# Attention maxima from score products of 32 rows per head, two heads side by side on TensorE

## The chip, the cores and the metric

The kernel runs on one core of a Trainium2 chip. The metric is the device time of one execution in microseconds (us). The core has TensorE for matrix products (PE; its weight loads are shown apart as PEld), VectorE (DVE), ScalarE (ACT), GpSimd (POOL) and SyncE (SP), which here issues all transfers. Engines run on their own and wait for each other through semaphores; each engine works through its own instructions in order, and SP's DMA issues are such instructions too.

## The reference, cut to what matters

```python
x = x + attention(layernorm(x))      # changed here
x = x + fp4_ffn(layernorm(x))
x = x + state_space(layernorm(x))
x = x + mixture_of_experts(layernorm(x))
# attention, x: (2, 1024, 128), 16 heads of 8 channels, rotary q and k
attn = jnp.einsum('bhqd,bhkd->bhqk', q, k) * scale
attn = jax.nn.softmax(attn, axis=-1)
out = jnp.einsum('bhqk,bhkd->bhqd', attn, v)
```

A softmax comes out the same whatever number is subtracted from a row's scores before the exponential, as long as it is near enough to the row's maximum.

## The kernel before, in words

q and k are split into three bf16 parts each and stored in DRAM (q_dram, k_dram). A stack of 72 rows, 3 x 3 pairs of parts x 8 channels, gives a float32-like score from one bf16 product; rows 72 to 95 of the stack add the negated row maximum, which is written into the stack of q later.

Attention runs in eight passes (PASSES), each of four heads (QUAD) of one batch entry, 1024 queries by 1024 keys. A pass has 16 steps (STEPS): two halves of the queries by eight key tiles of 128. In a step PE makes four transposed score products (L1310, keys on the partitions, 512 queries), ACT takes their exponentials (L738), and PE makes the value products of the step before (L1327; four heads, 16 columns each, side by side; float32, so each is two instructions).

The maxima for pass it+1 are made during pass it. Between the four products of a step PE puts the score products for two tiles (score_half, L1291; a tile is 128 queries of a head by 1024 keys, two products of 512), and DVE reduces each tile from two banks of PSUM (L970). Two tiles are in flight: PE waits for s_max before it overwrites banks. After 16 tiles DVE splits the 16 maxima into two bf16 parts and transposes them (L974 to L979), and SP writes them into the q stack with four small DMAs (store_maxima, L512). PE waits for them (s_nrow) ahead of step 0 for the first half and ahead of step 8 for the second. Before pass 0 the same tiles are made with nothing between them.

The stacks have three sets (SETS); set p is loaded again when its pass is over (load, L500 to L506: two loads into qs, six into ks and one small one). SP's queue in a pass is: maxima store for the next pass's first half; output store; wait for the end of the pass (s_pv); load; output store; maxima store for the next pass's second half. At the head of the program the stores of the first four part tiles are followed by the loads of all three sets, the other four part stores, and then the maxima stores of pass 0. After pass 5 SP goes on with load_out(0): the denominators den of the first batch entry, which DVE inverts (L987) ahead of its reductions for pass 7 (those that run during pass 6).

Of the kernel before, what the change touches and what calls it, by code (L numbers as in the profile page):

```python
# [14 lines left out]
BF16 = mybir.dt.bfloat16  # L15
F32R = mybir.dt.float32r
I32 = mybir.dt.int32
ALU = mybir.AluOpType
ACT = mybir.ActivationFunctionType
AX = mybir.AxisListType  # L20

P = 128
BATCH = 2
SEQ = 1024
# [3 lines left out]
BANK = 512  # L28
# [4 lines left out]
HD = D // HEADS  # L33
QUAD = 4
PASSES = BATCH * HEADS // QUAD
# [7 lines left out]
STEPS = 2 * KT  # L43
MAX_TILES = 2
SETS = 3
# [19 lines left out]
def build_kernel(nc, i, out):  # L65
# [3 lines left out]
    def sb(name, shape, dt=F32):  # L69
        return ctx.enter_context(nc.sbuf_tensor(name, shape, dt))  # L70

    def sem(name):
        return ctx.enter_context(nc.semaphore(name))

    with ctx:
        ps = ctx.enter_context(nc.psum_tensor("ps", [P, 8, BANK], F32))
# [4 lines left out]
        sq = sb("sq", [P, TILES, D])  # L81
# [42 lines left out]
        fill = sb("fill", [4 * (ROWS - PROD), 2, 2 * BANK], BF16)  # L124
        stacks = [[sb(f"{w}{n}", [ROWS, 2, QUAD, BANK], BF16) for w in ("qs", "ks")] for n in reversed(range(SETS))][::-1]
        qs, ks = ([pair[n] for pair in stacks] for n in range(2))
        prob = sb("prob", [P, 8, BANK])
        vq = [sb(f"vq{n}", [P, KT, QUAD, VW]) for n in range(SETS)]
        v = sb("v", [P, PASSES, KT, QC])
# [3 lines left out]
        bv_all = sb("bv_all", [P, D])  # L133
        bo_all = sb("bo_all", [P, D])
        nmax = sb("nmax", [P, 2, 16])
        nmax_p = sb("nmax_p", [P, 32], BF16)
        nmax_t = sb("nmax_t", [P, 2, 32], BF16)
        o_sb = sb("o_sb", [P, 2, BANK])
        den = sb("den", [P, BATCH, HEADS * SEQ // P])
        rden = sb("rden", [P, BATCH, SEQ])  # L140
        num = sb("num", [P, TOKENS])
        phase.close()

# [50 lines left out]
        q_dram = nc.dram_tensor("q_dram", (PASSES, 2, PARTS, QC, BANK), BF16, kind="Internal").ap()  # L194
# [30 lines left out]
        s_fill = sem("s_fill")  # L225
        s_set = sem("s_set")
        s_qk = [sem(f"s_qk{n}") for n in range(SETS)]
        s_score = sem("s_score")
        s_max = sem("s_max")
        s_nmax = sem("s_nmax")  # L230
# [113 lines left out]
        def norm_dve_var(k, h):  # L344
            a, b = h * TILES // 2, (h + 1) * TILES // 2
            nc.vector.wait_ge(s_squared, 2 * k + h + 1)
            nc.vector.tensor_reduce(stat[:, 2, a:b], sq[:, a:b, :], AX.X, ALU.add).then_inc(s_var, 1)  # L347

        def norm_dve_scale(k, h):
            a, b = h * TILES // 2, (h + 1) * TILES // 2  # L350
            u = 2 * k + h
            nc.vector.wait_ge(s_rstd, u + 1)
            nc.vector.wait_ge(s_centred, u + 1)
            nc.vector.tensor_tensor(xc[:, a:b, :], xc[:, a:b, :], bc(stat[:, 3, a:b], D),
                                    ALU.mult).then_inc(s_normed, 1)
# [81 lines left out]
        N_W34 = 3 + 16 + 6  # L437

        LOADS = 16 * (2 * (PARTS + 1) + 1)

        @block.sync
        def _(sp):
# [44 lines left out]
            def store_parts(u):  # L487
# [4 lines left out]
                for g in range(QUAD):  # L492
                    sp.dma_start(dst[4 * (c // 2) + g, c % 2].rearrange("n c t -> c n t"),
                                 parts[QC * g:QC * g + QC, u % CHUNKS]).then_inc(s_parts_out[u % CHUNKS], 16)

            def load(it, p):

                for f in range(2):

                    sp.dma_start(qs[p][0:PROD, f], q_dram[bass.ds(it, 1), f].rearrange(  # L500
                        "o n (d h) t -> (o n d) (h t)", h=QUAD).unsqueeze(1).to_broadcast([PARTS * HD, PARTS, QUAD * BANK])).then_inc(s_qk[p], 16)
                    for a in range(PARTS):
                        sp.dma_start(ks[p][HD * PARTS * a:HD * PARTS * (a + 1), f], k_dram[bass.ds(it, 1), f].rearrange(
                            "o n (d h) t -> d (o n) (h t)", h=QUAD)).then_inc(s_qk[p], 16)

                sp.dma_start(qs[p][PROD:PROD + 2], fill[0:16, 0, 0:BANK]).then_inc(s_qk[p], 16)  # L506
# [17 lines left out]
                sp.wait_ge(s_parts_out[n], 16 * QUAD)  # L524
            sp.wait_ge(s_set, 16 * 2 * SETS)
            for p in range(SETS):
                load(p, p)
            for u in range(CHUNKS, 2 * CHUNKS):
                store_parts(u)
# [5 lines left out]
            def one_pass(it, p, more, again=None):  # L535
                if more:
                    store_maxima(it + 1, (p + 1) % SETS, 0)
                store_out(it, 0)
                if again is not None:
                    sp.wait_ge(s_pv, STEPS * (it + 1))  # L540
                    load(again, p)
                store_out(it, 1)
                if more:
                    store_maxima(it + 1, (p + 1) % SETS, 1)
# [385 lines left out]
        def _(dve):  # L930
# [33 lines left out]
            def maxima(it):  # L964

                for half in range(2):
                    for n in range(16):
                        t = 16 * half + n
                        dve.wait_ge(s_score, 32 * it + t + 1)
                        nc.vector.tensor_reduce(nmax[:, half, n:n + 1], ps[:, 2 * (t % 2):2 * (t % 2) + 2, :],  # L970
                                                AX.XY, ALU.max, negate=True).then_inc(s_max, 1)
                    w = 2 * (2 * it + half)
                    dve.wait_ge(s_max, 32 * it + 16 * half + 16)
                    nc.vector.tensor_copy(nmax_p[:, 0:16], nmax[:, half]).then_inc(s_mstep, 1)  # L974
                    dve.wait_ge(s_mstep, w + 1)
                    nc.vector.tensor_tensor(nmax_p[:, 16:32], nmax[:, half], nmax_p[:, 0:16], ALU.subtract).then_inc(s_mstep, 1)
                    dve.wait_ge(s_mstep, w + 2)
                    dve.wait_ge(s_nrow[half], 64 * it)
                    nc.vector.transpose(nmax_t[:, half, :], nmax_p[:]).then_inc(s_nmax, 1)  # L979

# [25 lines left out]
            dve.wait_ge(s_res, 2)  # L1006
            norm_dve_a(1, 0)
            dve.wait_ge(s_qk[SETS - 1], LOADS * (PASSES // SETS + 1))
            quant(0, wf[:], wfq[:], (s_wf, 16 * 5), scaled=lambda: norm_dve_var(1, 0), before_last=lambda: norm_dve_scale(1, 0))
            quant(1, x_half(xc, 0), x_half(sq, 0), (s_normed, 3))  # L1010

# [241 lines left out]
        def _(pe):  # L1253
# [29 lines left out]
                                          start=True, stop=True)  # L1283
                mm.then_inc(s_v_ps, 1)

            def score_half(it, p, t, kk):

                half, h, q = t // 16, t % 16 // 4, t % 4
                if kk == 0 and not (isinstance(it, int) and it == 0 and t < 2):
                    pe.wait_ge(s_max, 32 * it + t - 1)  # L1290
                mm = nc.tensor.matmul(ps[:, 2 * (t % 2) + kk], qs[p][:, half, h, q * P:(q + 1) * P],  # L1291
                                      ks[p][:, kk, h, :], start=True, stop=True)
                if kk == 1:
                    mm.then_inc(s_score, 1)

            def one_pass(it, p, first, more, loads=None, between={}):
                for s in range(STEPS):
                    if s in between:
                        between[s]()
                    half, kt = divmod(s, KT)  # L1300
                    if kt == 0:
                        pe.wait_ge(s_nrow[half], 64 * (it + 1))
                    if more and s == 0:
                        pe.wait_ge(s_qk[(p + 1) % SETS], LOADS * loads)
                    todo = [(MAX_TILES * s + n // 2, n % 2) for n in range(2 * MAX_TILES)] if more else []
                    for j in range(QUAD):
                        n = 4 * s + j
                        if n >= 3:
                            pe.wait_ge(s_exp, 4 * STEPS * it + n - 2)
                        nc.tensor.matmul(ps[:, 4 + (first + n) % 3], ks[p][:, kt // 4, j, kt % 4 * P:(kt % 4 + 1) * P],  # L1310
                                         qs[p][:, half, j, :], start=True, stop=True).then_inc(s_st, 1)
                        for t, kk in todo[len(todo) * j // 4:len(todo) * (j + 1) // 4]:
                            score_half(it + 1, (p + 1) % SETS, t, kk)
                        if s >= 1 and j == (QUAD - 1 if more else QUAD - 2):
                            products(it, p, s - 1)
                products(it, p, STEPS - 1)
# [11 lines left out]
                                          start=(kt == 0), stop=(kt == KT - 1))  # L1328
                mm.then_inc(s_pv, 1)

            pe.wait_ge(s_qk[0], LOADS)
            pe.wait_ge(s_v, 4)
            for t in range(32):
                score_half(0, 0, t, 0)
                score_half(0, 0, t, 1)
            with pe.Fori(0, PASSES // SETS) as r:
                for p in range(SETS):
                    one_pass(SETS * r + p, p, 4 * STEPS * p, True, r + 1 + (p + 1) // SETS)
            one_pass(PASSES - 2, 0, 0, True, PASSES // SETS + 1)

            def project_out(b):

# [68 lines left out]
                pe.wait_ge(s_wft, 3)  # L1411
                turn_x(1, 1)

            one_pass(PASSES - 1, 1, 4 * STEPS, False, between={1: lambda: project_out(0), 8: turn_weights, 12: turn_first_x})
            pe.wait_ge(s_wft, 3)
            for p in range(4):
                gate_up(p)
# [239 lines left out]
```

## Time and profile before

| | |
|---|---|
| median of 3 runs | 1059.84 us (1059.75 to 1062.03) |
| the profiled execution | 1058.78 us, span 1057.0 us |
| busy | PE 82%, DVE 82%, ACT 54%, POOL 23% of the span |
| attention | from about 41 us (first load of a stack) to 471 us |

The span is from the first to the last instruction. A timeline row shows start, duration, engine, line and operation, how many instructions are merged into it, and in brackets the engine's idle time ahead of it with what ended it. A matmul's duration is modelled and overlaps its successors: for the rate of PE one reads the distance between starts. Rows with SPq are DMA issues in SP's queue, the time that SP needs to hand the transfer over, not the transfer itself.

### The profile page before, as it was taken

The numbers are of one execution on the slowest core, as the hardware profiler recorded it, in microseconds if no ns is written. First come the engines' busy times: TensorE is split into PE (matmuls) and PEld (weight loads), VectorE is DVE, ScalarE is ACT, GpSimd is POOL, SyncE is SP. The second block draws the span as 40 slices with busy tenths as digits, with TensorE's granted clock in tenths as the row PEclk, the third lists the DMA queues.
The fourth block names the chain that finished last, engine by engine and source line by source line (L and its number), as shares of the span: only waits on it lengthen the run. The fifth ranks groups of instructions, "written<-read, shape, count | busy, mean of one in ns | idle before, by whom it ended". The sixth has DMA issues, their size and how long they took to land. (4 is left out here: it accounts for less than half of the span.)

```text
span 1057.0 us, 12554 instructions
## 1 busy us (share of the span) xinstructions
PE 862.0 (82%) x3703; PEld 392.3 (37%) x3703; DVE 862.0 (82%) x795; ACT 572.5 (54%) x897; POOL 238.8 (23%) x131
## 2 busy tenths in 40 slices
PE   5589999989999949985464457777777579999998
PEld 2212222222222212224342222222222266888886
DVE  6698888878888748828956899999999873888886
ACT  2304777767777737882131642332333165888885
POOL 3700000000000000100110156776777620123110
PEclk9857999999999979998677788998999867999999
DMA  7440020110101030003000233444444002122111
GB/s 174 128 132 1 11 56 24 54 58 12 56 11 57 14 99 11 11 20 85 0 1 0 89 119 118 160 158 140 158 159 158 21 1 83 60 97 83 60 60 41
DMA packets 37977, 73.51 MB, mean 70 GB/s; under 512 B 7299, under 2 KB 21627, under 8 KB 36891
## 3 DMA queue, kind: packets, MB, share of 16 engines
q1 hardware_dynamic: 37922, 72.82, 21.7%
q8 instruction: 30, 0.49, 0.2%
q14 instruction: 25, 0.20, 0.1%
HBM read 62.50 MB, written 8.85 MB: 68 GB/s over the span
## 5 line engine op out<-in xcount | busy, mean ns | idle before, releaser
L970 DVE TENSOR_REDUCE nmax<-ps 128x1 f32<-128x1024 f32 x256 | 301.0, 1218 | 57.3 <-PE ps L1291 57.3
L738 ACT ACTIVATE prob<-ps 128x512 f32<-128x512 f32 x512 | 265.7, 605 | 137.1 <-PE ps L1310 136.8
L1291 PE MATMUL ps<-ks,qs 96*128 96x512 bf16 x512 | 206.3, 416 | 29.7 <-DVE nmax L970 18.1
L1310 PE MATMUL ps<-qs,ks 96*128 96x512 bf16 x512 | 194.7, 389 | 7.0 <-ACT prob L738 3.3
L670 POOL TENSOR_TENSOR hc<-hst,cbr 128x1024 f32<-128x1024 f32 x64 | 153.4, 2398 | 93.1 <-DVE hst L1107 93.1
L1489 PE MATMUL ps<-hc,ident 128*128 128x512 f32 x256 | 134.4, 650 | 41.7 <-POOL hc L670 38.8
L862 ACT ACTIVATE ps<-dt,a_neg 128x1024 f32<-128x1024 f32 x64 | 71.5, 1118 | 145.9 <-DVE hst L1107 145.9
L1107 DVE TENSOR_TENSOR_SCAN hst<-ps,dbx 128x1024 f32<-128x1024 f32 x64 | 145.6, 2276 | 0.0
L1327 PE MATMUL ps<-prob,vq 128*16 128x512 f32 x1024 | 133.6, 598 | 0.8 <-ACT prob L738 0.7
L1174 DVE TENSOR_TENSOR act_l<-act_t,act_h 128x1024 fp32r<-128x1024 f32 x64 | 92.1, 1449 | 35.5 <-ACT act_h L903 35.5
L1310 PEld LDWEIGHTS ps<-qs,ks 96*128 96x128 bf16 x512 | 49.6, 98 | 164.6 <-ACT prob L738 117.5
L899 ACT ACTIVATE act_t<-ps,b_now 128x512 f32<-128x512 f32 x128 | 82.8, 683 | 24.1 <-PE ps L1531 24.1
L1489 PEld LDWEIGHTS ps<-hc,ident 128*128 128x128 f32 x256 | 47.1, 202 | 106.6 <-POOL hc L670 67.8
L1291 PEld LDWEIGHTS ps<-ks,qs 96*128 96x128 bf16 x512 | 48.9, 101 | 100.8 <-DVE nmax L970 53.0
L1096 DVE TENSOR_TENSOR dbx<-dtx,ps 128x1024 f32<-128x1024 f32 x64 | 76.3, 1193 | 3.2 <-PE ps L1476 3.1
L903 ACT ACTIVATE act_h<-act_t 128x1024 fp32r<-128x1024 f32 x64 | 67.9, 1061 | 2.0
L644 POOL COPY vq<-v 128x256 f32<-128x256 f32 x8 | 3.1, 403 | 272.8 <-PE ps L1327 272.8
L377 POOL TENSOR_SCALAR stat<-stat 128x8 f32<-128x8 f32 x8 | 4.2, 525 | 265.2 <-DVE stat L347 265.1
L1476 PE MATMUL ps<-bcp,sel_b 128*128 128x512 bf16 x128 | 41.2, 405 | 21.5 <-DVE dbx L1096 19.7
L1529 PE MATMUL ps<-xh,w_l 128*128 128x512 f32 x128 | 51.7, 404 | 0.0
L1530 PE MATMUL ps<-xl,w_h 128*128 128x512 f32 x128 | 51.2, 400 | 0.0
L1531 PE MATMUL ps<-xh,w_h 128*128 128x512 f32 x128 | 51.1, 400 | 0.0
(176 smaller groups left out, 969.7 us busy)
## 6 DMA issues: line engine op xcount, KB each, us to landing
cbr<-s_dram SPq DMA_DIRECT2D x64, 512.0 KB, 3.6
gate<-c_dram SPq DMA_DIRECT2D x8, 1024.0 KB, 6.7
qs<-q_dram SPq DMA_DIRECT2D x18, 288.0 KB
ks<-k_dram SPq DMA_DIRECT2D x54, 96.0 KB
o_dram<-o_sb SPq DMA_DIRECT2D x16, 256.0 KB, 2.1
wf<-in_L_ffn_w SPq DMA_DIRECT2D x8, 256.0 KB, 2.8
wfq<-in_L_ffn_w SPq DMA_DIRECT2D x8, 256.0 KB, 3.1
q_dram<-parts SPq DMA_DIRECT2D x16, 96.0 KB, 2.1
```

The costliest lines, as they stand in the source:

```text
L670: nc.gpsimd.tensor_tensor(hc[:, slot], hst[:, slot], cbr[:, slot], ALU.mult).then_inc(s_hc, 1)
L738: nc.scalar.activation(prob[:, n % 8], ps[:, 4 + (first + n) % 3], ACT.Exp, scale=ATT_SCALE).then_inc(s_exp, 1)
L862: nc.scalar.activation(abar(slot), dt[:, b * SEQ:(b + 1) * SEQ], ACT.Exp, scale=a_neg[:, bass.ds(n, 1)]).then_inc(s_abar, 1)
L899: nc.scalar.activation(act_t[:, u % 2, h], ps[:, h], ACT.Gelu, bias=b1_now[:, u // CHUNKS, h:h + 1]).then_inc(s_gelu, 1)
L970: nc.vector.tensor_reduce(nmax[:, half, n:n + 1], ps[:, 2 * (t % 2):2 * (t % 2) + 2, :], AX.XY, ALU.max, negate=True).then_inc(s_max, 1)
L1096: nc.vector.tensor_tensor(dbx[:, slot].rearrange("p (k t) -> p k t", k=2), dtx[:, b * SEQ:(b + 1) * SEQ].rearrange("p (k t) -> p k t", k=2 ...
L1107: nc.vector.tensor_tensor_scan(hst[:, slot], abar(slot), dbx[:, slot], 0.0, ALU.mult, ALU.add).then_inc(s_scan, 1)
L1174: nc.vector.tensor_tensor(act_l[:, u % 2, h:h + 2], act_t[:, u % 2, h:h + 2], act_h[:, u % 2, h:h + 2].bitcast(F32), ALU.subtract).then_in ...
L1291: mm = nc.tensor.matmul(ps[:, 2 * (t % 2) + kk], qs[p][:, half, h, q * P:(q + 1) * P], ks[p][:, kk, h, :], start=True, stop=True)
L1310: nc.tensor.matmul(ps[:, 4 + (first + n) % 3], ks[p][:, kt // 4, j, kt % 4 * P:(kt % 4 + 1) * P], qs[p][:, half, j, :], start=True, stop=T ...
L1327: mm = nc.tensor.matmul(ps[32 * j:32 * j + VW, 7], vq[p][:, kt, j, :], prob[:, (4 * s + j) % 8], start=(kt == 0), stop=(kt == KT - 1))
L1489: mm = nc.tensor.matmul(ps[:, 6 + k], ident[:], hc[:, slot, k * BANK:(k + 1) * BANK], start=first, stop=last)
```

## The change

The products from which the maxima are made use only the two leading parts of q and k: 2 x 2 pairs x 8 channels = 32 rows for a head. They get operands of their own, qm and km (128 partitions, four heads of 32 rows under one another). score_pair makes two products, for two heads that lie on neighbouring groups of 32 rows of TensorE, into two banks; DVE reduces each bank for itself (two maxima for each reduction), and the two halves of the keys are joined by one further small operation. The scores that go into the exponential still come from the stacks of 96 rows. The order of tiles changes from head by head to query tile by query tile.

The operands come by a new function load_heads: for each half of the sequence and each head one DMA into km and two into qm, 24 in all, ahead of each load. PE waits for s_qm instead of s_qk ahead of the maxima's products, and for s_qk at the start of a pass. rden takes the place of sq, to make room.

```diff
+        qm, km = ([sb(f"{w}{n}", [P, 2, BANK], BF16) for n in range(SETS)] for w in ("qm", "km"))
+            def load_heads(it, p):
+
+                for f in range(2):
+                    for h in range(QUAD):
+                        q, k = (t[bass.ds(it, 1), f].rearrange("o n (d h) t -> (o n d) h t", h=QUAD)[0:2 * HD, h]
+                                for t in (q_dram, k_dram))
+                        sp.dma_start(km[p][32 * h:32 * h + 32, f], k.unsqueeze(0).to_broadcast([2, 2 * HD, BANK])).then_inc(s_qm[p], 16)
+                        for a in range(2):
+                            sp.dma_start(qm[p][32 * h + 16 * a:32 * h + 16 * a + 16, f],
+                                         q[HD * a:HD * a + HD].unsqueeze(0).to_broadcast([2, HD, BANK])).then_inc(s_qm[p], 16)
...
             for p in range(SETS):
+                load_heads(p, p)
                 load(p, p)
...
                     sp.wait_ge(s_pv, STEPS * (it + 1))
+                    load_heads(again, p)
                     load(again, p)
...
-                        nc.vector.tensor_reduce(nmax[:, half, n:n + 1], ps[:, 2 * (t % 2):2 * (t % 2) + 2, :],
-                                                AX.XY, ALU.max, negate=True).then_inc(s_max, 1)
+                        nc.vector.tensor_reduce(nmax_k[:, half, kk, 2 * pair:2 * pair + 2, qt], ps[:, 2 * pair:2 * pair + 2, :],
+                                                AX.X, ALU.max, negate=True).then_inc(s_max, 1)
...
+                    nc.vector.tensor_tensor(nmax[:, half], nmax_k[:, half, 0].rearrange("p h q -> p (h q)"),
+                                            nmax_k[:, half, 1].rearrange("p h q -> p (h q)"), ALU.min).then_inc(s_mstep, 1)
...
-                mm = nc.tensor.matmul(ps[:, 2 * (t % 2) + kk], qs[p][:, half, h, q * P:(q + 1) * P],
-                                      ks[p][:, kk, h, :], start=True, stop=True)
+                for n in range(2):
+                    rows = slice(32 * (2 * pair + n), 32 * (2 * pair + n + 1))
+                    mm = nc.tensor.matmul(ps[:, 2 * pair + n], qm[p][rows, half, qt * P:(qt + 1) * P],
+                                          km[p][rows, kk, :], start=True, stop=True)
+                mm.then_inc(s_score, 1)
...
-                        for t, kk in todo[len(todo) * j // 4:len(todo) * (j + 1) // 4]:
-                            score_half(it + 1, (p + 1) % SETS, t, kk)
+                        if more and j % 2:
+                            score_pair(it + 1, (p + 1) % SETS, MAX_TILES * s + j // 2)
```

PE, one step inside a pass. Before (L1310 are the four products for the exponentials, L1291 those for the maxima, L1327 the value products):

```order
L1310 MATMUL ps<-qs,ks 128x512 [waits s_exp]
L1290 REGISTER_ALU
L1291 MATMUL ps<-ks,qs 128x512 [waits s_max]
L1309 REGISTER_ALU
L1310 MATMUL ps<-qs,ks 128x512 [waits s_exp]
L1291 MATMUL ps<-ks,qs 128x512
L1327 MATMUL ps<-prob,vq 16x512 [waits s_exp]
L1327 MATMUL ps<-prob,vq 16x512 x3
```

Now (L1333 are the products for the exponentials, L1315 the pair for the maxima, L1350 the value products):

```order
L1333 MATMUL ps<-qs,ks 128x512 [waits s_exp]
L1332 REGISTER_ALU
L1333 MATMUL ps<-qs,ks 128x512 [waits s_exp]
L1312 REGISTER_ALU
L1315 MATMUL ps<-km,qm 128x512 [waits s_max]
L1315 MATMUL ps<-km,qm 128x512
L1350 MATMUL ps<-prob,vq 16x512 [waits s_exp]
L1350 MATMUL ps<-prob,vq 16x512 x3
```

The products for the maxima stood one by one between the others; now two stand together after every second one, and the wait for DVE is ahead of each pair.

SP, from the end of a pass to the store of the second half's maxima. Before:

```order
L500 ISA [waits s_pv]
L500 DMA qs<-q_dram 72x1x2048
L503 DMA ks<-k_dram 24x1x2048 x3
L500 ISA
L500 DMA qs<-q_dram 72x1x2048
L503 DMA ks<-k_dram 24x1x2048 x3
L506 DMA qs<-fill 2x8x512
L518 ISA [waits s_o]
L518 DMA o_dram<-o_sb 128x512
L512 DMA qs<-nmax_t 2x16x32 [waits s_nmax]
L512 DMA qs<-nmax_t 2x16x32 x3
```

Now (the five rows from the second on come eight times, and then what stood there before):

```order
L506 ISA [waits s_pv]
L506 DMA km<-k_dram 32x1x512
L508 DMA qm<-q_dram 16x1x512
L508 ISA
L508 DMA qm<-q_dram 16x1x512
L506 ISA
...
L515 DMA qs<-q_dram 72x1x2048
L518 DMA ks<-k_dram 24x1x2048 x3
...
L533 DMA o_dram<-o_sb 128x512
L527 DMA qs<-nmax_t 2x16x32 [waits s_nmax]
```

24 issues with their register instructions stand between the end of the pass and the nine loads, and so ahead of the maxima's stores too. At the head of the program the same 24 stand ahead of the loads of each of the three sets.

## Rows read from the trace of the kernel before

**Rows 1.** Timeline of PE in one step (start us, us, engine, line, operation, count).
```profile
200.84 0.39 PE L1310 MATMUL ps<-qs,ks 96*128 96x512 bf16 x1
...
202.36 0.38 PE L1291 MATMUL ps<-ks,qs 96*128 96x512 bf16 x1
202.67 1.05 PE L1327 MATMUL ps<-prob,vq 128*16 128x512 f32 x8
203.65 0.39 PE L1310 MATMUL ps<-qs,ks 96*128 96x512 bf16 x1
```

**Rows 2.** Timeline of DVE in the same stretch.
```profile
201.91 2.36 DVE L970 TENSOR_REDUCE nmax<-ps 128x1 f32<-128x1024 f32 x2 [0.46 <-PE ps L1291]
...
204.51 0.18 DVE L976 TENSOR_TENSOR nmax_p<-nmax,nmax_p 128x16 bf16<-128x16 f32 x1
```

**Rows 3.** Timeline of ACT in the same stretch.
```profile
201.27 2.07 ACT L738 ACTIVATE prob<-ps 128x512 f32<-128x512 f32 x4 [0.75 <-PE ps L1310]
```

**Rows 4.** Timeline of PE: first products of passes 1, 2, 3; step 8 of 3.
```profile
135.99 0.39 PE L1310 MATMUL ps<-qs,ks 96*128 96x512 bf16 x1
...
181.54 0.39 PE L1310 MATMUL ps<-qs,ks 96*128 96x512 bf16 x1
...
229.88 0.39 PE L1310 MATMUL ps<-qs,ks 96*128 96x512 bf16 x1 [2.72 <-issue]
...
253.06 0.39 PE L1310 MATMUL ps<-qs,ks 96*128 96x512 bf16 x1
```

**Rows 5.** Timeline of SP's queue after pass 5 (SPq: the issue of a DMA).
```profile
367.93 0.90 SPq L500 DMA_DIRECT2D qs<-q_dram  x1
368.93 2.32 SPq L503 DMA_DIRECT2D ks<-k_dram  x3
371.45 0.81 SPq L500 DMA_DIRECT2D qs<-q_dram  x1
...
375.63 0.35 SPq L518 DMA_DIRECT2D o_dram<-o_sb  x1
376.10 2.67 SPq L512 DMA_DIRECT2D qs<-nmax_t  x4
379.03 0.66 SPq L551 DMA_DIRECT2D den<-o_dram  x1
...
384.67 0.53 SPq L556 DMA_DIRECT2D rden<-r_dram  x1
```

**Rows 6.** Page, parts 3 (packets, MB, share) and 6 (KB, us to landing).
```profile
q1 hardware_dynamic: 37922, 72.82, 21.7%
...
o_dram<-o_sb SPq DMA_DIRECT2D x16, 256.0 KB, 2.1
```

**Rows 7.** Timeline of SP's queue at the head of the program.
```profile
49.07 2.08 SPq L503 DMA_DIRECT2D ks<-k_dram  x3
51.19 0.79 SPq L500 DMA_DIRECT2D qs<-q_dram  x1
...
61.50 1.88 SPq L493 DMA_DIRECT2D q_dram<-parts  x4
...
71.41 0.66 SPq L512 DMA_DIRECT2D qs<-nmax_t  x1
```

**Rows 8.** Timeline of PE: first score product, starts of passes 0 and 6.
```profile
50.76 1.46 PE L1291 MATMUL ps<-ks,qs 96*128 96x512 bf16 x3 [9.67 <-DMA qs<-fill]
...
88.57 0.63 PE L1310 MATMUL ps<-qs,ks 96*128 96x512 bf16 x1
...
367.60 0.39 PE L1310 MATMUL ps<-qs,ks 96*128 96x512 bf16 x1
...
383.46 0.61 PE L1291 MATMUL ps<-ks,qs 96*128 96x512 bf16 x1 [13.70 <-DVE nmax L970]
```

**Rows 9.** Timeline of DVE after pass 5.
```profile
381.37 0.95 DVE L987 RECIPROCAL den<-den 128x128 f32<-128x128 f32 x1 [13.35 <-DMA den<-o_dram]
```

**Rows 10.** Page, part 2: granted clock in tenths, 40 slices.
```profile
PEclk9857999999999979998677788998999867999999
```

More of the change, by code:

```diff
@@ L135, in build_kernel @@
         nmax = sb("nmax", [P, 2, 16])
+        nmax_k = sb("nmax_k", [P, 2, 2, QUAD, 4])
         nmax_p = sb("nmax_p", [P, 32], BF16)
@@ L139, in build_kernel @@
         den = sb("den", [P, BATCH, HEADS * SEQ // P])
-        rden = sb("rden", [P, BATCH, SEQ])
+        rden = sq[:].rearrange("p (b t) c -> p b (t c)", b=BATCH)
         num = sb("num", [P, TOKENS])
@@ L227, in build_kernel @@
         s_qk = [sem(f"s_qk{n}") for n in range(SETS)]
+        s_qm = [sem(f"s_qm{n}") for n in range(SETS)]
         s_score = sem("s_score")
@@ L439, in build_kernel @@
         LOADS = 16 * (2 * (PARTS + 1) + 1)
+        HEAD_LOADS = 16 * 2 * 3 * QUAD
         @block.sync
@@ L967, in maxima @@
                     for n in range(16):
-                        t = 16 * half + n
-                        dve.wait_ge(s_score, 32 * it + t + 1)
-                        nc.vector.tensor_reduce(nmax[:, half, n:n + 1], ps[:, 2 * (t % 2):2 * (t % 2) + 2, :],
-                                                AX.XY, ALU.max, negate=True).then_inc(s_max, 1)
-                    w = 2 * (2 * it + half)
+                        u = 16 * half + n
+                        qt, kk, pair = n // 4, n % 4 // 2, n % 2
+                        dve.wait_ge(s_score, 32 * it + u + 1)
+                        nc.vector.tensor_reduce(nmax_k[:, half, kk, 2 * pair:2 * pair + 2, qt], ps[:, 2 * pair:2 * pair + 2, :],
+                                                AX.X, ALU.max, negate=True).then_inc(s_max, 1)
+                    w = 3 * (2 * it + half)
                     dve.wait_ge(s_max, 32 * it + 16 * half + 16)
+                    nc.vector.tensor_tensor(nmax[:, half], nmax_k[:, half, 0].rearrange("p h q -> p (h q)"),
+                                            nmax_k[:, half, 1].rearrange("p h q -> p (h q)"), ALU.min).then_inc(s_mstep, 1)
+                    dve.wait_ge(s_mstep, w + 1)
                     nc.vector.tensor_copy(nmax_p[:, 0:16], nmax[:, half]).then_inc(s_mstep, 1)
-                    dve.wait_ge(s_mstep, w + 1)
+                    dve.wait_ge(s_mstep, w + 2)
                     nc.vector.tensor_tensor(nmax_p[:, 16:32], nmax[:, half], nmax_p[:, 0:16], ALU.subtract).then_inc(s_mstep, 1)
-                    dve.wait_ge(s_mstep, w + 2)
+                    dve.wait_ge(s_mstep, w + 3)
                     dve.wait_ge(s_nrow[half], 64 * it)
@@ L1284, in _, with score_pair, one_pass @@
                 mm.then_inc(s_v_ps, 1)
[L1286 to L1290, printed above, removed]
-                mm = nc.tensor.matmul(ps[:, 2 * (t % 2) + kk], qs[p][:, half, h, q * P:(q + 1) * P],
-                                      ks[p][:, kk, h, :], start=True, stop=True)
-                if kk == 1:
-                    mm.then_inc(s_score, 1)
-            def one_pass(it, p, first, more, loads=None, between={}):
+            def score_pair(it, p, u):
+                half, qt, kk, pair = u // 16, u % 16 // 4, u % 4 // 2, u % 2
+                if not (isinstance(it, int) and it == 0 and u < 2):
+                    pe.wait_ge(s_max, 32 * it + u - 1)
+                for n in range(2):
[3 more added lines that the diff above has]
+                mm.then_inc(s_score, 1)
+            def one_pass(it, p, first, loads, more, between={}):
+                pe.wait_ge(s_qk[p], LOADS * loads)
                 for s in range(STEPS):
@@ L1303, in one_pass @@
                     if more and s == 0:
-                        pe.wait_ge(s_qk[(p + 1) % SETS], LOADS * loads)
-                    todo = [(MAX_TILES * s + n // 2, n % 2) for n in range(2 * MAX_TILES)] if more else []
+                        pe.wait_ge(s_qm[(p + 1) % SETS], HEAD_LOADS * (loads + (p + 1) // SETS))
                     for j in range(QUAD):
@@ L1329, in products @@
                 mm.then_inc(s_pv, 1)
-            pe.wait_ge(s_qk[0], LOADS)
+            pe.wait_ge(s_qm[0], HEAD_LOADS)
             pe.wait_ge(s_v, 4)
-            for t in range(32):
-                score_half(0, 0, t, 0)
-                score_half(0, 0, t, 1)
+            for u in range(32):
+                score_pair(0, 0, u)
             with pe.Fori(0, PASSES // SETS) as r:
                 for p in range(SETS):
-                    one_pass(SETS * r + p, p, 4 * STEPS * p, True, r + 1 + (p + 1) // SETS)
-            one_pass(PASSES - 2, 0, 0, True, PASSES // SETS + 1)
+                    one_pass(SETS * r + p, p, 4 * STEPS * p, r + 1, True)
+            one_pass(PASSES - 2, 0, 0, PASSES // SETS + 1, True)
             def project_out(b):
@@ L1412, in turn_first_x @@
                 turn_x(1, 1)
-            one_pass(PASSES - 1, 1, 4 * STEPS, False, between={1: lambda: project_out(0), 8: turn_weights, 12: turn_first_x})
+            one_pass(PASSES - 1, 1, 4 * STEPS, PASSES // SETS + 1, False, between={1: lambda: project_out(0), 8: turn_weights, 12: turn_first_x})
             pe.wait_ge(s_wft, 3)
```

1 line of the change is left out of this document (added).

## The prediction

> **What bounds the kernel now.** I read the page's slices first (the clock is full through attention but for slice 3 and the stops [rows 10]), then the order of time on PE and DVE in the middle of an attention pass, then SP's own queue around a pass boundary, since the change puts most of its new instructions there.
>
> A steady step of a pass takes 2.81 us on PE (200.84 to 203.65): eight products of 96 rows, then the value products, then the next step's first product [rows 1]. Products in the same mode start 0.217 us apart (200.84 to 202.36 is seven of them). In that stretch PE never sits idle, while DVE waits 0.46 us for PE before each pair of reductions, and its two reductions take 2.36 us [rows 2]. ACT's four exponentials fit easily (2.07 us of work with a wait of 0.75 us for PE ahead of them) [rows 3]. So PE is the bound inside a pass, DVE is 0.46 us behind it, and a shorter PE step is worth something until DVE stops it. A pass is 16 steps, 45.55 us from first product to first product (135.99 to 181.54), and its step 8 comes 22.11 us after its start (181.54 to 203.65) [rows 4, 1].
>
> SP is nobody's bound before, but look at when it is asked. After a pass ends it issues the loads for a set three passes on, and only behind them, in the same queue, the last four stores of the maxima of the pass that is already running. PE needs those at step 8. At the boundary into pass 6, PE starts at 367.60, the loads start at 367.93 and the fourth maxima store is issued at 378.1 (376.10, four in 2.67 us) [rows 8, 5]. A small store lands 2.1 us after its issue, by the o_dram row [rows 6]; so the maxima are there 12.6 us after the start of the pass, 9.5 us before step 8. That slack is what the change spends.
>
> Two places have no slack. At the head of the program the stores of pass 0's maxima stand behind all three sets of loads (first maxima store 71.41) [rows 7]; PE starts pass 0 at 88.57 [rows 8]. And between passes 5 and 6 PE stands 13.70 us, because DVE waits 13.35 us for the denominators, whose load SP issues at 379.03, behind the same loads and stores [rows 8, 9, 5].
>
> **The score products.** 512 products of 96 rows go; 512 of 32 rows come, two at a time on different row groups. If a pair runs side by side, a step has two product slots fewer, 0.43 us. But the pair and its neighbours differ in how they occupy the array. The rows show what a change of mode costs: from the last 96-row product to the value products (16 columns each) 0.31 us instead of 0.22 (202.36 to 202.67) [rows 1], so 0.09 us. The new order alternates two ordinary products, a pair, two ordinary products, a pair; three more changes in a step. Step: 2 x 0.217 (within the ordinary products) + 4 x 0.31 (into or out of a pair) + 0.01 (within the pairs; the value products, eight in 1.05 us, start as close together) + 0.98 (value products to the next step) = 2.66 us, 0.15 less than 2.81. No row shows 32-row products. With no price for the three new changes the step would be 2.39, which is also about where DVE stops it (2.36 us for the two reductions [rows 2]); if the two of a pair ran one after the other, it would be 3.09. I take 2.66.
>
> The Trainium skill (TensorEngine Tiling (Array Packing), Key Properties) says that changing the tiling mode, not just the tile, drains TensorE; that speaks against this order, and the 0.31 above agrees. By TensorE: Matmul & The Clock Gate (Part 3) products on different row groups start some 4 ns apart, which gives 2.66 with the drain and 2.39 without; no row here shows it for rows.
>
> **DVE.** 256 reductions stay, each over 1024 elements, and write two maxima instead of one; same duration. One more small operation for each half pass, 16 in all, like the 0.18 us subtraction [rows 2]. It falls into DVE's 0.46 us of idle time per step, or behind SP; zero. If that cover were gone it would be 3 us.
>
> **The new loads.** Each set gets 24 more DMAs, 8 into km (32 x 512) and 16 into qm (16 x 512), issued ahead of the nine that were there. What an issue costs SP: the ks loads, nearest in form (one row per partition, source dims that don't match the destination's), take 2.12 us for three at the head (49.07 to 51.19), 0.71 each [rows 7], and inside the loop with the address register 2.52 for three (368.93 to 371.45), 0.84 each [rows 5]. So a block of 24 is 17.0 us at the head and 20.2 us in the loop. Bounds: the issue of rden (0.53, where a ks load's alone is 0.67: 2.08 for three with two gaps of 0.04) [rows 5, 7], the part stores (1.88 for four, 0.47) [rows 7] and the o_dram store (0.35) [rows 5] below; the qs loads (0.90) above. I take the ks row.
>
> Head of the program: 3 x 17.0 = 51.0 us on SP. The first maxima store moves from 71.41 to 122.4, the fourth is issued at 124.4 and lands at 126.5. PE's own start slips only by 17.0 instead of 7.2 us (its first product waited for the nine loads until 50.76 [rows 8]), and 88.57 + 9.8 = 98.4 is early enough to be hidden. Pass 0 starts at 126.5 instead of 88.57: **+37.9**.
>
> Pass 0: 15 steps x 0.15: **-2.3** (its first step has no value products, and saves nothing to speak of).
>
> Passes 1, 2, 4, 5: maxima for step 8 land 12.6 + 20.2 = 32.8 us after the start; PE is ready for step 8 at 22.11 - 1.1 = 21.0, so it stands 11.8 us. What is left of the pass is 45.55 - 22.11 - 8 x 0.15 = 22.2 us. After a stop the clock is low for a while: pass 3 starts after a stop at 229.88 and reaches step 8 at 253.06, 23.2 instead of 22.1, so 1.1 us [rows 4]. Period 32.8 + 22.2 + 1.1 = 56.1, against 45.55: +10.55 each, **+42.2**. The saving of the first eight steps is swallowed by the wait.
>
> Pass 3: the same, but the 2.72 us for instructions at the loop's end and the 1.1 behind it [rows 4] lie in the time that is now waited anyway: 10.55 - 3.8, **+6.8**.
>
> Pass 6: its maxima are no trouble, as it already stands. But the denominators' load is issued behind the (unused) loads of pass 5, so DVE, and PE with it, start 20.2 later: 20.2 - 2.3 = **+17.9**.
>
> Pass 7 has no score products, and pass 6 issues no loads: 0. Everything behind attention moves as a block.
>
> Sum: 37.9 - 2.3 + 42.2 + 6.8 + 17.9 = +102.5. The profiled execution took 1058.78 us (span 1057.0): 1161.3. The median of the three runs is 1.1 higher: **1162 us**. 216 new issues lie on the path (72 at the head, 24 at each of six boundaries), so 0.01 us in the price of one is 2.2 us of the result.
>
> **Rivals.**
> Cheap issues: the new DMAs have plain row counts, and cost SP what the part stores or the o_dram store do, 0.2 to 0.32 less than I took. Even then 24 x 0.52 + 12.6 = 25.1 is beyond step 8. 216 x 0.2 = 43, 216 x 0.32 = 69: 1093 to 1119 us.
> Pairs one after the other: 0.43 more in each of 70 steps that count (15 in passes 0 and 6, 8 in the five others): +30, 1192 us.
> Few DMA engines: a block is 512 packets of 1 KB. The program's mean packet is 1.9 KB and holds an engine for 97 ns (21.7% of 16 x 1057 us by 37922) [rows 6]. On sixteen engines that is nothing. If a DMA used only two, it would be 256 packets each: 13 us if time goes with size, hidden behind SP; 25 us if it doesn't, then 7.8 more for each of three blocks and 4.6 for each of six: +51, 1213 us. The skill's page DMA: Bandwidth & Descriptors (How many engines) gives two here, as the source's slowest dimension is the repeated 2; no row shows the number of engines.
> Clock: pauses or half-empty products keep PE at 1.2 GHz after each stop; as it stood at the head, 5 tenths in slice 3 [rows 10]. 70 steps of some 4.9 us: +157, 1318 us. Against it: after the stop before pass 3 it cost 1.1 us in all.
> Faster: if an issue costs 0.27 all in, a block takes 6.5 us, the maxima arrive at 19.1, before step 8 even of a 2.39 us step (22.11 - 7 x 0.42 = 19.2), and the wait of passes 1 to 5 is gone. Then seven passes give 7 x 15 x 0.42 = 44, less 6.4 at the head (71.41 + 19.5 + 4.1 = 95.0) and 6.5 before pass 6: 1028 us. At 0.35 the waits are back with 1.8 + 1.1 us in five passes and the gain is some 10; the sign turns at about 0.39 from start to start. The cheapest row of such a queue is the o_dram store, 0.35 for the issue and 0.46 with the register move before the next [rows 5].
>
> **How the numbers follow.** Forecast 0.68, cheap issues 0.10, pairs in series 0.10, few engines 0.05, clock 0.04, faster 0.03. The forecast's own spread is 1162 less 30 (0.53 for an issue) less 19 (step 2.39), and up some 20 (0.09 more for an issue). The range 1112 to 1195 takes in that, the upper edge of cheap issues and pairs in series. About 0.2% (2 us) is what a measurement can tell; faster by more 0.03, within 0.01, slower 0.96.
>
> **What would show it.** SP: km and qm issues of 0.67 us, and the first maxima store at about 122. PE: a start of pass 0 near 126, stops of some 12 us at step 8 of passes 1, 2, 4 and 5 that end with the maxima's stores, a stop of some 33 us before pass 6; spacings of 0.31 around each pair and almost none in it. DVE waits, where it was nearly the bound. It is wrong if issues are 0.4 us or less, if PE waits at step 8 for nothing, or if pass 0 starts before 110.

## The result, and the profile after

The changed kernel takes 1167.8 us (median; 1163.9 to 1169.9), the kernel before 1060.3 in the same runs: ratio 1.101, 95% interval 1.097 to 1.104. The profiled execution has a span of 1164.2 us against 1057.0. The forecast was 1162 us with a range of 1112 to 1195.

Where the 107.2 us of span went, from the first products of the passes in the two traces:

| stretch | before | after | difference | forecast |
|---|---|---|---|---|
| start of pass 0 | 88.57 | 121.70 | +33.1 | +37.9 |
| pass 0 | 47.42 | 46.94 | -0.5 | -2.3 |
| pass 1 | 45.55 | 56.07 | +10.5 | +10.55 |
| pass 2 (with the loop's end) | 48.34 | 60.02 | +11.7 | +10.55 |
| pass 3 | 46.62 | 55.77 | +9.2 | +6.8 |
| passes 4 and 5 | 91.10 | 115.31 | +24.2 | +21.1 |
| pass 6 | 60.55 | 78.78 | +18.2 | +17.9 |
| from pass 7 to the end | 628.9 | 629.6 | +0.8 | 0 |

First the step on PE, the timeline of two steps of pass 2 (start us, us, engine, line, operation, count); it answers to [rows 1].

```profile
240.39 0.60 PE L1333 MATMUL ps<-qs,ks 96*128 96x512 bf16 x2
240.92 0.39 PE L1315 MATMUL ps<-km,qm 32*128 32x512 bf16 x2
241.24 0.61 PE L1333 MATMUL ps<-qs,ks 96*128 96x512 bf16 x2
241.79 0.39 PE L1315 MATMUL ps<-km,qm 32*128 32x512 bf16 x2
242.10 1.05 PE L1350 MATMUL ps<-prob,vq 128*16 128x512 f32 x8
243.09 0.60 PE L1333 MATMUL ps<-qs,ks 96*128 96x512 bf16 x2
```

The two 32-row products of a pair are given 0.39 us together, as much as one 96-row product alone in [rows 1]: the pair runs side by side. From a pair's start to what follows it is 0.32 us (240.92 to 241.24, 241.79 to 242.10). The step is 2.70 us, against 2.81. DVE in the same stretch still waits for PE, now 0.34 us instead of the 0.46 of [rows 2]:

```profile
241.35 2.36 DVE L988 TENSOR_REDUCE nmax_k<-ps 128x2 f32<-128x1024 f32 x2 [0.34 <-PE ps L1315]
```

SP's queue behind pass 1, cut (it answers to [rows 5]):

```profile
224.99 0.70 SPq L506 DMA_DIRECT2D km<-k_dram  x1
225.80 1.49 SPq L508 DMA_DIRECT2D qm<-q_dram  x2
...
244.34 0.83 SPq L515 DMA_DIRECT2D qs<-q_dram  x1
...
252.29 5.37 SPq L527 DMA_DIRECT2D qs<-nmax_t  x8
```

24 issues take 19.35 us (224.99 to 244.34), and the maxima's stores, four of which pass 2 needs at step 8, begin at 252.29, 27.6 us after the pass began at 224.71. What PE makes of that at step 8 of pass 1, with the stop in brackets; behind it the same instructions at half the clock (granted 0.51 from 199 to 205 us, 1.00 from 205 to 208):

```profile
188.73 1.05 PE L1350 MATMUL ps<-prob,vq 128*16 128x512 f32 x8
199.75 1.03 PE L1333 MATMUL ps<-qs,ks 96*128 96x512 bf16 x2 [9.96 <-DMA qs<-nmax_t]
200.72 0.60 PE L1315 MATMUL ps<-km,qm 32*128 32x512 bf16 x2
201.25 1.03 PE L1333 MATMUL ps<-qs,ks 96*128 96x512 bf16 x2
202.22 0.61 PE L1315 MATMUL ps<-km,qm 32*128 32x512 bf16 x2
202.75 1.91 PE L1350 MATMUL ps<-prob,vq 128*16 128x512 f32 x8
204.60 0.73 PE L1333 MATMUL ps<-qs,ks 96*128 96x512 bf16 x2
```

At the head and ahead of pass 6, timelines of PE, SP and DVE; they answer to [rows 7 to 9]:

```profile
121.70 1.03 PE L1333 MATMUL ps<-qs,ks 96*128 96x512 bf16 x2 [25.65 <-DMA qs<-nmax_t]
```
```profile
117.81 5.23 SPq L527 DMA_DIRECT2D qs<-nmax_t  x8
```
```profile
490.95 0.61 PE L1315 MATMUL ps<-km,qm 32*128 32x512 bf16 x2 [32.51 <-DVE nmax_k L988]
```
```profile
488.86 0.95 DVE L1008 RECIPROCAL den<-den 128x128 f32<-128x128 f32 x1 [32.42 <-DMA den<-o_dram]
```

PE had finished the head's products and stood 25.65 us for stores that SP issued at 117.81 instead of 71.41. The stop that the prediction puts before pass 6 lies inside its first step, in both traces (before: pass 6 starts at 367.60, the stop ends at 383.46; now 455.81 and 490.95); it grew from 13.70 to 32.51 us.

The stores themselves are not slow. Once four of them are issued, PE goes on: the fourth of the eight in the row at 252.29 is issued at about 254.3 and PE's step 8 of pass 2 begins at 256.22; at the head it is about 119.8 and 121.70. Both times 1.9 us, in pass 2 right behind 33 loads.

```profile
256.22 1.03 PE L1333 MATMUL ps<-qs,ks 96*128 96x512 bf16 x2 [10.36 <-DMA qs<-nmax_t]
```

### The profile page after: what moved, and what is told of

Same layout as the page of the kernel before. It is cut to its first block and busy times, and to the rows that moved or that the text cites. A ratio compares the mean times of both kernels' runs of the same rounds, so it can differ in the third digit from the quotient of the medians.

```text
span 1164.2 us, 13027 instructions
## 1 busy us (share of the span) xinstructions
PE 860.2 (74%) x3701; PEld 368.2 (32%) x3703; DVE 865.5 (74%) x811; ACT 572.6 (49%) x897; POOL 238.8 (21%) x131
## 5 line engine op out<-in xcount | busy, mean ns | idle before, releaser
L988 DVE TENSOR_REDUCE nmax_k<-ps 128x2 f32<-128x1024 f32 x256 | 300.7, 1220 | 140.2 <-PE ps L1315 140.2
L1333 PE MATMUL ps<-qs,ks 96*128 96x512 bf16 x512 | 171.8, 411 | 77.4 <-DMA qs<-nmax_t 69.8
L1315 PE MATMUL ps<-km,qm 32*128 32x512 bf16 x512 | 111.5, 435 | 67.7 <-DVE nmax_k L988 49.9
L1350 PE MATMUL ps<-prob,vq 128*16 128x512 f32 x1024 | 142.7, 636 | 0.8 <-ACT prob L755 0.7
L1333 PEld LDWEIGHTS ps<-qs,ks 96*128 96x128 bf16 x512 | 39.6, 98 | 245.4 <-issue 124.9
L1315 PEld LDWEIGHTS ps<-km,qm 32*128 32x128 bf16 x512 | 24.4, 93 | 169.0 <-issue 81.1
L1498 PE MATMUL ps<-bcp,sel_b 128*128 128x512 bf16 x126 | 40.8, 406 | 22.2 <-DVE dbx L1118 20.0
```

The source lines that it names most:

```text
L988: nc.vector.tensor_reduce(nmax_k[:, half, kk, 2 * pair:2 * pair + 2, qt], ps[:, 2 * pair:2 * pair + 2, :], AX.X, ALU.max, negate=True).the ...
L1315: mm = nc.tensor.matmul(ps[:, 2 * pair + n], qm[p][rows, half, qt * P:(qt + 1) * P], km[p][rows, kk, :], start=True, stop=True)
L1350: mm = nc.tensor.matmul(ps[32 * j:32 * j + VW, 7], vq[p][:, kt, j, :], prob[:, (4 * s + j) % 8], start=(kt == 0), stop=(kt == KT - 1))
```

## The experiments

The theory: the loss is nothing but SP's issue time of the new DMAs at three kinds of place (head, step 8, denominators), while the products themselves gain a little, as far as the changes of mode let them. Rivals: the products or the low clock carry the loss; the transfers and not their issue do; the 0.3 us beside a pair are not the change of mode. Each run was timed beside the kernel before.

### The loads alone

The kernel before, with operands, load_heads and its calls of the change, and nobody reading them.

```diff
             for p in range(SETS):
+                load_heads(p, p)
                 load(p, p)
...
+                    load_heads(again, p)
                     load(again, p)
```

> The kernel before with the 24 new DMAs issued ahead of each load of a set, into operands that nobody reads; the score products stay as they were. Theory (the loss is SP's issue time ahead of the maxima's stores and the denominators): pass 0 starts at about 122 us instead of 88.6, passes 1, 2, 4, 5 take 57.7 us each (stores land 31.9 us after their start, then 23.4 us of steps and 2.4 us of low clock), the stop before pass 6 is 33 us; about 1171 us, even a little more than the changed kernel, as the steps stay at 2.81 us. Rival (the 32-row products or the clock carry a good part of the loss): well under 1150 us.

Measured: 1165.9 us, ratio 1.101 (1.097 to 1.104). Pass 0 starts at 120.96, pass 1 takes 56.83 us (not the 57.7 forecast, as the issues take 0.81 instead of 0.84; passes 4 and 5 take 57.6 and 58.0), and PE's stop at its step 8 reads:

```profile
188.75 0.38 PE L1309 MATMUL ps<-ks,qs 96*128 96x512 bf16 x1
189.06 1.05 PE L1345 MATMUL ps<-prob,vq 128*16 128x512 f32 x8
199.18 0.60 PE L1328 MATMUL ps<-qs,ks 96*128 96x512 bf16 x1 [9.07 <-DMA qs<-nmax_t]
199.58 0.63 PE L1309 MATMUL ps<-ks,qs 96*128 96x512 bf16 x1
```

The whole loss is there without one 32-row product, and the low clock behind the stop comes with 96-row products too (granted 0.61 from 199 to 205 us). The rival of the products falls.

### The products alone

The changed kernel without the DMAs; qm and km hold a constant, so that the maxima of the rows are left out.

```diff
-                load_heads(p, p)
...
-                    load_heads(again, p)
...
+            for t in (*qm, *km):
+                ins = nc.gpsimd.memset(t[:], 1.375)
```

> The changed kernel without any of the new DMAs: qm and km are filled once with a constant, so the subtracted maxima are not the rows' own; every product, reduction and store of maxima is made as in the change. Theory: steps of 2.70 instead of 2.81 us, no stops at step 8, the head and the stop before pass 6 as in the kernel before: 7 passes x 1.45 us and some 2 us in the head, about 1048 us. Rival (changing the mode costs nothing by itself, the 0.31 us are waits for something that the loads delay): steps of 2.4 us, about 1016 us. Rival (the products lose time of their own): 1060 us or more.

Measured: 1053.5 us, ratio 0.995 (0.992 to 0.997). The direction is that of the theory and neither rival's; the size is 6.4 instead of 12 us. Steps are 2.70 us and pass 1 takes 43.90 instead of 45.55; pass 0 keeps nothing of that (47.39 against 47.42 us), since its first steps ran at the low clock for longer (two steps of 3.0 and 4.85 us and 3.25 for the third, against 3.4, 3.7 and 2.8 before). In the trace, the fastest of the ten executions, pass 7 starts at 420.63 instead of 428.15, 7.5 us earlier. Of the 0.11 us that a step saves, step 9 of a pass gives 0.10 back: it takes 2.98 us at full clock and without a stop, against 2.88 before.

```profile
190.53 0.60 PE L1333 MATMUL ps<-qs,ks 96*128 96x512 bf16 x2
191.07 0.39 PE L1315 MATMUL ps<-km,qm 32*128 32x512 bf16 x2
191.39 0.61 PE L1333 MATMUL ps<-qs,ks 96*128 96x512 bf16 x2
191.94 0.39 PE L1315 MATMUL ps<-km,qm 32*128 32x512 bf16 x2
192.25 1.05 PE L1350 MATMUL ps<-prob,vq 128*16 128x512 f32 x8
193.24 0.60 PE L1333 MATMUL ps<-qs,ks 96*128 96x512 bf16 x2
```

The spacings are those of the changed kernel though no new DMA runs: they belong to PE.

### Stores ahead of loads

```diff
-                if again is not None:
-                    sp.wait_ge(s_pv, STEPS * (it + 1))
-                    load_heads(again, p)
-                    load(again, p)
                 store_out(it, 1)
                 if more:
                     store_maxima(it + 1, (p + 1) % SETS, 1)
+                if again is not None:
+                    sp.wait_ge(s_pv, STEPS * (it + 1))
+                    load_heads(again, p)
+                    load(again, p)
```

> The changed kernel; at a pass's end SP stores the output and the second half's maxima first and issues the 24 new and 9 old loads behind them. Theory: the stops at step 8 go with the low clock behind them, 12.5 us in each of passes 1, 2, 4, 5 and about 7.5 in pass 3, while the head and the stop before pass 6 stay: about 1110 us. Rival (the transfers themselves, not their issue, hold the stores back): the stops stay in part and the time is above 1140 us.

Measured: 1106.1 us, ratio 1.044 (1.040 to 1.047). The bytes are the same and so is the number of DMAs; only who stands behind whom differs. SP's queue behind pass 0 and PE at step 8 of pass 1 (191.24), without a stop:

```profile
171.54 2.63 SPq L527 DMA_DIRECT2D qs<-nmax_t  x4
174.46 0.69 SPq L506 DMA_DIRECT2D km<-k_dram  x1
```
```profile
190.26 1.05 PE L1350 MATMUL ps<-prob,vq 128*16 128x512 f32 x8
191.24 0.60 PE L1333 MATMUL ps<-qs,ks 96*128 96x512 bf16 x2
```

Passes 1, 4 and 5 take 43.9 us each (pass 1: 170.17 to 214.07), no more than in the products alone, though all the new transfers run in them. Pass 3 takes 49.3 against 46.4 there, with a granted clock of 0.52 from 260 to 274 us behind the stop at the loop's end; why it stayed low for longer is open. 62 us of the 107 were this place. By itself the new order would also have freed stores that stood behind transfers and not behind issues; that rival falls by the 1.9 us from issue to PE in the changed kernel, shown above.

### The head's order

```diff
+            load_heads(0, 0)
+            load(0, 0)
+            load_heads(1, 1)
+            sp.wait_ge(s_qk[0], LOADS)
+            store_maxima(0, 0, 0)
+            load(1, 1)
+            store_maxima(0, 0, 1)
             for u in range(CHUNKS, 2 * CHUNKS):
                 store_parts(u)
+            load_heads(2, 2)
+            load(2, 2)
```

> The changed kernel; at the head SP issues only what pass 0 needs (set 0, and the new operands of set 1) ahead of pass 0's maxima stores, and the rest behind. Theory: pass 0 starts at about 97 us, when the head's reductions are through, instead of 121.7: about 1143 us. Rival (PE's pass 0 waits for something else there, such as the transfers): no more than 10 us gained, 1158 us or more.

Measured: 1144.5 us, ratio 1.080 (1.076 to 1.084). Pass 0 starts at 95.44, right behind the last product of the head:

```profile
93.77 0.60 PE L1319 MATMUL ps<-km,qm 32*128 32x512 bf16 x2 [0.52 <-DVE nmax_k L992]
94.91 0.61 PE L1319 MATMUL ps<-km,qm 32*128 32x512 bf16 x2 [0.53 <-DVE nmax_k L992]
95.44 1.03 PE L1337 MATMUL ps<-qs,ks 96*128 96x512 bf16 x2
```

The start of pass 0 comes 26.3 us earlier than in the changed kernel, and 23 us of the whole came back by order alone (1167.8 to 1144.5). The 6.9 us that are left of the 33.1 go with the later first product, 59.3 instead of 50.8, for which the first block has to be issued anyway.

### Half the loads

As the loads alone, with `for h in range(2)` in load_heads: 12 new DMAs a block.

> The kernel before with 12 instead of 24 unread new DMAs ahead of each load (those of two heads). Theory (issue time against a slack): in the loop 12 issues are 9.7 us, the stores land 22.3 us after the start of the pass against step 8 at 22.1, so passes 1 to 5 lose next to nothing; the head loses about 11 us and the stop before pass 6 grows by 9.7: about 1081 us. Rival (each DMA costs its share wherever it stands): half the loss of the 24, about 1113 us.

Measured: 1078.5 us, ratio 1.017 (1.014 to 1.019). Half of the DMAs cost a sixth of the 24's loss (17 of 106 us). PE has no stop at step 8 in any of passes 1 to 5, which together take 231.7 us against 231.6 before. What is lost lies where there was no slack: in the trace pass 6 starts 9.6 us later, and its first two steps take 30.24 instead of 20.28 us. The cost is not one for each DMA; it starts where the slack ends.

### The new DMAs off SP's queue

GpSimd issues all blocks but the 16 DMAs that the head's first products need; SP stores maxima first, the loads after pass 5 that nobody reads are gone, and the first denominators are fetched after pass 4. SP's loop over the passes is written out, so that its addresses are constants.

```diff
+            def heads(it, p):
+                for f in range(2):
+                    heads_k(nc.gpsimd, it, p, f, s_qm[p])
+                    heads_q(nc.gpsimd, it, p, f, s_qm[p])
...
+            for it in range(SETS, PASSES):
+                pool.wait_ge(s_pv, STEPS * (it - SETS + 1))
+                values(it, it % SETS)
+                heads(it, it % SETS)
```

> The change with its new DMAs taken off SP's queue: GpSimd, idle in attention, issues them (SP only the 16 that the head's first products need). SP stores the maxima ahead of loads, the loads that nobody reads after pass 5 are gone, and the first denominators are fetched a pass earlier. Theory (only SP's issue time cost something): no stops at step 8 or before pass 6, pass 0 starts at about 91 us, steps of 2.70 us: the 1053.5 us of the products alone, less 15 for the stop before pass 6, plus some 1.5 at the head: about 1040 us. Rival (the transfers, or GpSimd's slower issue, cost time themselves): 1050 us or more.

Measured: 1037.9 us, ratio 0.978 (0.974 to 0.982), faster than both kernels. Pass 0 starts at 89.81. GpSimd's own timeline at the head:

```profile
46.84 4.68 POOL L456 DMA_DIRECT2D qm<-q_dram  x8
51.45 0.46 POOL L671 COPY vq<-v 128x256 f32<-128x256 f32 x1
51.80 2.39 POOL L450 DMA_DIRECT2D km<-k_dram  x4
```

An issue took it 0.58 us (4.68 by 8), no more than SP's. The passes between the stops take what they take in the products alone (pass 1: 43.90), so neither the transfers nor GpSimd's issues cost anything there.

### The same queue for the kernel before

Only the new order, the dropped loads, the earlier denominators and the written-out loop, none of the change. At the head two sets and not one are loaded ahead of the maxima's stores, as pass 0 reads both.

> The kernel before with the same order of SP's queue (maxima stores ahead of loads, no unread loads, first denominators fetched a pass earlier), nothing of the change. Theory: only the stop before pass 6 goes, 15 us with the low clock behind it: about 1045 us, so the change's products are worth 5 to 7 us over it. Rival (the order of the queue is what helps at other places too): under 1040 us, and no gain is left for the products.

Measured: 1043.4 us, ratio 0.982 (0.979 to 0.986). So three quarters of what the version above gains over the kernel before has nothing to do with the change. In the trace the first two steps of pass 6 take 5.35 instead of 20.28 us. The change is worth 5.5 us between the two medians; the intervals of the two ratios overlap, but the slowest of the four executions with the change (1040.7 us) is faster than the fastest of the four without (1042.2 us).

### One change of mode more, one less

Both on GpSimd's queue. One more: the pairs stand after the first and the third ordinary product.

```diff
-                        if more and j % 2:
+                        if more and j % 2 == 0:
```

> As the one with GpSimd's queue, but the pairs stand after the first and the third ordinary product: six changes of mode in a step instead of five, the same products. Theory (each change costs PE 0.09 us): steps of 2.79 us, +9.5 us, about 1049 us. Rival (the 0.31 us next to a pair is the pair's own length, not the change): steps of 2.70 us, no difference to 1040 us.

Measured: 1046.1 us, ratio 0.985 (0.981 to 0.989), 8.2 us more than with five changes. The step:

```profile
195.05 0.39 PE L1354 MATMUL ps<-qs,ks 96*128 96x512 bf16 x1
195.37 0.39 PE L1336 MATMUL ps<-km,qm 32*128 32x512 bf16 x2
195.69 0.60 PE L1354 MATMUL ps<-qs,ks 96*128 96x512 bf16 x2
196.23 0.39 PE L1336 MATMUL ps<-km,qm 32*128 32x512 bf16 x2
196.55 0.39 PE L1354 MATMUL ps<-qs,ks 96*128 96x512 bf16 x1
196.87 1.05 PE L1371 MATMUL ps<-prob,vq 128*16 128x512 f32 x8
197.85 0.39 PE L1354 MATMUL ps<-qs,ks 96*128 96x512 bf16 x1
```

Same products, 2.80 us (195.05 to 197.85), and no wait among them: the order costs 0.10 us for one change more. The rival, that 0.32 us is a pair's own length, falls.

One less: both pairs together after the second ordinary product.

```diff
-                        if more and j % 2:
-                            score_pair(it + 1, (p + 1) % SETS, MAX_TILES * s + j // 2)
+                        if more and j == 1:
+                            score_pair(it + 1, (p + 1) % SETS, MAX_TILES * s)
+                            score_pair(it + 1, (p + 1) % SETS, MAX_TILES * s + 1)
```

> As the one with GpSimd's queue, but both pairs of a step stand together after its second ordinary product: four changes of mode in a step instead of five, and the second pair on the two other row groups. Theory: PE alone would need 2.39 us for a step, but both pairs then wait for DVE nearly at once; stepping through the two waits gives steps that alternate between 2.35 and 2.81 us, 2.58 on average: about 1028 us. Rival (the two waits add up in each step): steps of 2.81 us or more, 1050 us.

Measured: 1038.6 us, ratio 0.978 (0.975 to 0.982), no difference to five changes; the forecast of 1028 was a miss. The steps do alternate as worked out:

```profile
164.82 0.60 PE L1354 MATMUL ps<-qs,ks 96*128 96x512 bf16 x2
165.35 0.40 PE L1336 MATMUL ps<-km,qm 32*128 32x512 bf16 x4
165.68 0.60 PE L1354 MATMUL ps<-qs,ks 96*128 96x512 bf16 x2
166.22 1.05 PE L1372 MATMUL ps<-prob,vq 128*16 128x512 f32 x8
167.20 0.60 PE L1354 MATMUL ps<-qs,ks 96*128 96x512 bf16 x2
167.74 0.85 PE L1336 MATMUL ps<-km,qm 32*128 32x512 bf16 x4
168.52 0.61 PE L1354 MATMUL ps<-qs,ks 96*128 96x512 bf16 x2
169.05 1.05 PE L1372 MATMUL ps<-prob,vq 128*16 128x512 f32 x8
170.04 0.61 PE L1354 MATMUL ps<-qs,ks 96*128 96x512 bf16 x2
```

2.38 us with four products in 0.40 (165.35: four row groups at once), then 2.84 where the second pair waits for DVE. But some steps of each pass took more than with the pairs apart: steps 0 and 1 together 5.22 instead of 4.86 us, step 9 3.23 instead of 2.98, the last step 3.87 instead of 3.57. That is 0.9 of the 1.6 us that the other twelve steps gain, and pass 5 took 43.20 instead of 43.84 us. In passes 1 and 4 the low clock took the rest and more (44.8 instead of 43.9 us each): steps 0 and 1 of pass 1 took 6.51 us, with a granted clock of 0.57 from 140 to 144 us, where the version with five changes has 1.00. At the start of pass 7 the trace is 0.8 us ahead, and the medians show nothing of it.

### Together, but not behind the waits

Pairs together in steps 2 to 7 and 10 to 15, apart in the others (`together = s % KT >= 2`).

> As the one with GpSimd's queue; the pairs stand together in steps 2 to 7 and 10 to 15 of a pass and apart in the two steps behind each wait for maxima, where the version with all pairs together had a step of 3.2 us and, behind some pass starts, the low clock. Theory (that version's gain of 0.09 us a step was lost only there): 12 steps x 0.09 in each of seven passes, about 1030 us. Rival (DVE, busy all the time then, takes the gain back at the small operations between the halves): 1036 us or more.

Measured: 1030.2 us, ratio 0.971 (0.969 to 0.973): the fastest of all, and its interval lies clear of the 0.979 to 0.986 of the kernel before with the new queue. Pass 1 takes 42.92 us instead of the 43.90 with the pairs apart, 0.98 where the forecast had 12 x 0.09. Together with this order and GpSimd's queue the change is worth some 13 us (1043.4 to 1030.2; the two were timed in different sessions, in which the kernel before took 1061.2 and 1061.6).

## Why the prediction was right

By its own steps. *Issue time at the head*: mechanism and place were right; the term was a little large (37.9 for 33.1). An issue took 0.65 us from start to start instead of the ks loads' 0.71, 72 x 0.06 = 4.3 us, and SP's wait between the part stores and the first maxima store was 1.6 us instead of 2.3.

*Step 8*: right in place and nearly in size. Pass 1 can be set against the sum. PE was ready 21.1 us after the start (forecast 21.0) and stood 10.0 us (forecast 11.8): the block took 19.35 instead of 20.2 us, the stores were there 1.9 instead of 2.1 us after their issue, and the rest is spread. What was left of the pass took 22.8 us at full clock (forecast 22.2), as a step saves 0.11 us and not 0.15, and step 9 only takes 0.10 more than before. The low clock took 2.15 us (forecast 1.1). So a stop 1.8 us too long was made good by two terms 0.6 and 1.05 us too small: that pass 1 came out at +10.5 for +10.55 is luck in the last digit.

*Low clock behind a stop*: the one term that was clearly mis-sized. 1.1 us was taken from the short stop ahead of pass 3. Against the same steps at full clock (2.70, and 2.98 for step 9) it came to 2.15 us in pass 1 (a step of 4.85), 2.7 in pass 2, 4.5 in pass 4 (4.85, 4.85 and 3.14) and 2.6 in pass 5. Why it differs from pass to pass no run shows.

*Pass 3*: +9.2 instead of +6.8. The clock was low behind the 3.02 us stop ahead of the pass, from 286.45 to 297 us, and again behind the 3.42 us stop at step 8; the first stretch was swallowed by the wait at step 8, the second cost 4.2 us. *Pass 0*: -0.5 instead of -2.3, as the steps saved 0.11 and not 0.15 us and the low clock behind the longer stop took 3.0 us of its first two steps, against 1.9 before. *Denominators*: right within 0.3 us. *The pair*: right; 2.70 for 2.66, which is 0.32 instead of 0.31 into or out of a pair.

The rivals. Cheap issues fell with 0.62 us against the ks loads' 0.67; pairs in series fell with two products in 0.39 us; the clock came back after each stop. Few DMA engines: no row shows their number, but the transfers kept up. In the 20 us from 225 to 245, while a block was issued, the 16 engines were busy for 9% on average, 29 us of one engine's time; an estimate from that: even on two engines it would be 14 us each, less than the 19.35 us of the issues.

The loads alone cost 106 us and the products alone gain 6. The two do not add up: 106.0 - 6.4 is 99.6, and the change costs 107.5. Two things in the traces account for most of the 7.9 us. The wait at step 8 swallows what the eight steps ahead of it save in five passes (5 x 8 x 0.11 = 4.4 us), as the prediction says; and the low clock behind the stops at step 8 took 16.1 us in passes 1 to 5 of the changed kernel and 13.3 with the loads alone.

## What to carry to other kernels

A queue that nobody waits for may have a deadline all the same: before putting issues into it, measure from what is needed back to when it is asked for (here 12.6 of 22.1 us), and count issues, not bytes: the store of 256 KB took SP 0.35 us to issue [rows 5, 6], a load of 16 KB 0.6 us. Half of the new DMAs fitted into that slack and cost next to nothing in the loop. What is needed soonest goes ahead of what is needed three passes on, and an idle engine's queue is a place for the rest. Where products of different tiling alternate on TensorE, group them by kind: each change cost some 0.1 us here.

## What the runs showed of the hardware

- Two products on neighbouring groups of 32 rows, 512 columns each, take 0.39 us together, and four on four groups 0.40 us; from the first of them to the next 96-row product it is 0.32 and 0.33 us.
- A change between 96-row products, pairs of 32-row products and products of 16 columns costs 0.09 to 0.10 us; six in place of five changes made the step 2.80 instead of 2.70 us.
- SP needs 0.60 to 0.62 us to issue a DMA of 16 or 32 rows of 1 KB, 0.65 from start to start with fixed addresses and 0.81 with one from a register (19.35 us by 24). GpSimd needs 0.58.
- A stop of 10 us was followed by 5 to 10 us at 1.2 GHz, although PE has no gap in them (granted 0.51 from 199 to 205 us in pass 1, 0.50 from 371 to 380 us in pass 4), and stops of 3.0 and 3.4 us in pass 3 by as much; with the pairs together the clock fell in pass 1 with no stop ahead of it but one of 0.42 us.
- A store of 2 KB let PE go on 1.9 us after its issue, right behind the issue of 33 loads.
